# Cross attention's first loads in another order, the latent weights' split one slot later, and pair 0's mask product last

## The reference

```
xn     = layernorm(x)
scores = xn @ ctx^T / sqrt(512)         # 64 x 256 per batch
scores = where(mask, scores, -1e30)
x1     = x + softmax(scores) @ ctx      # 0 where a batch has no valid row
z      = layernorm(x1) @ [wq_a; wkv_a]^T    # latent projection, 512 -> 576
z      = z + bias, then rmsnorm and rope of its parts
```

## Time and profile before

| what | value |
|---|---|
| median of 3 runs | 1119.59 us (1118.59 to 1121.09) |
| profiled execution, first to last instruction | 1117.5 us |
| TensorE busy | 1087.1 us, 97% of the span |
| VectorE, ScalarE, GpSimd busy | 532.0, 348.9, 324.1 us |
| cross attention | about the first 130 us, slots of 8.12 us from slot 5 on |

### The profile page before, as it was taken

How to read it: one execution, slowest core, us unless ns; L and a number is a source line. 1 busy time by engine, 2 the same in 40 slices (tenths; PEclk the granted TensorE clock), 3 DMA queues, 4 the chain that set the end, 5 groups by cost and what they waited for, 6 DMA issues and landing times.

```text
span 1117.5 us, 20885 instructions
## 1 busy us (share of the span) xinstructions
PE 1087.1 (97%) x8097; PEld 948.6 (85%) x8097; DVE 532.0 (48%) x998; ACT 348.9 (31%) x698; POOL 324.1 (29%) x371
## 2 busy tenths in 40 slices
PE   5999999999999999999999999999999999999996
PEld 3677787888988898888988888889999998989895
DVE  3666556544454444434443456745344443525242
ACT  3555554322222222232222225513122222313130
POOL 2334470121212121121212122525243332415151
PEclk9999999999999999999999999999999999999998
DMA  9999942002011111102111117401010010101000
GB/s 355 414 418 381 407 184 70 22 18 75 20 42 47 42 56 41 48 19 69 30 33 56 39 52 232 170 1 39 1 39 22 17 38 0 38 0 39 1 19 19
DMA packets 41071, 100.96 MB, mean 90 GB/s; under 512 B 7289, under 2 KB 11412, under 8 KB 36532
## 3 DMA queue, kind: packets, MB, share of 16 engines
q1 hardware_dynamic: 39284, 96.62, 24.4%
q10 hardware_dynamic: 1728, 3.54, 0.8%
HBM read 74.45 MB, written 17.30 MB: 82 GB/s over the span
## 4 chain that ended last, share of the span: by engine, by line
PE 90%; DVE 3%; issue 2%; POOL 2%; DMA 1%; ACT 1%; SPq 0%; DVEq 0%; POOLq 0%; ACTq 0%
PE b_z L44 6%; PE b_z L45 6%; PE b_z L46 6%; PE b_score L44 5%; PE b_prob L46 5%; PE b_prob L44 5%; PE b_score L46 5%; PE b_score L45 5%; PE b_prob L45 5%; PE b_z L1101 3%; PE b_read L44 3%; PE b_free L44 3%; PE b_read L46 2%; PE b_read L45 2%; PE b_free L46 2%; PE b_free L45 2%
## 5 line engine op out<-in xcount | busy, mean ns | idle before, releaser
L817 POOL TENSOR_TENSOR m_e<-m_e,m_rs 128x512 f32<-128x512 f32 x32 | 34.6, 1083 | 357.8 <-DVE m_rs L972 357.8
L1447 POOL TENSOR_TENSOR f_hT_lo<-f_h,f_hT_hi 128x512 fp32r<-128x512 f32 x64 | 89.4, 1397 | 93.3 <-ACT f_hT_hi L1490 88.5
L46 PE MATMUL b_z<-m_zT_hi,m_wq_hi 128*128 128x256 f32 x384 | 108.7, 283 | 0.0
L44 PE MATMUL b_z<-m_zT_lo,m_wq_hi 128*128 128x256 f32 x384 | 108.7, 283 | 0.0
L45 PE MATMUL b_z<-m_zT_hi,m_wq_lo 128*128 128x256 f32 x384 | 108.7, 283 | 0.0
L1546 DVE TENSOR_TENSOR f_h<-f_h 128x512 f32<-128x512 f32 x64 | 72.7, 1136 | 61.4 <-ACT f_h L1485 61.4
L913 DVE TENSOR_TENSOR m_pT_lo<-b_turn,m_pT_hi 128x512 fp32r<-128x512 f32 x32 | 22.1, 692 | 160.3 <-ACT m_pT_hi L864 160.3
L858 ACT ACTIVATE m_qT<-b_z,m_q_bias 128x256 f32<-128x256 f32 x128 | 53.7, 471 | 79.0 <-PE b_z L46 75.3
L44 PEld LDWEIGHTS b_z<-m_zT_lo,m_wq_hi 128*128 128x128 f32 x384 | 73.7, 192 | 0.0
L45 PEld LDWEIGHTS b_z<-m_zT_hi,m_wq_lo 128*128 128x128 f32 x384 | 73.7, 192 | 0.0
L46 PEld LDWEIGHTS b_z<-m_zT_hi,m_wq_hi 128*128 128x128 f32 x384 | 73.7, 192 | 0.0
(11 more groups left out here) (234 smaller groups left out, 3176.9 us busy)
## 6 DMA issues: line engine op xcount, KB each, us to landing
x_ctx_in<-ctx_rows_dram SPq DMA_DIRECT2D x16, 1024.0 KB, 15.3
x_ctxT<-ctx_turned_dram SPq DMA_DIRECT2D x15, 1024.0 KB, 14.9
m_swapped<-m_by_sin SPq DMA_DIRECT2D x128, 64.0 KB, 2.0
m_raw<-attn_raw_dram SPq DMA_DIRECT2D x6, 768.0 KB, 11.0
m_z_in<-z_scratch SPq DMA_DIRECT2D x8, 576.0 KB, 3.8
x_x_all<-x_dram SPq DMA_DIRECT2D x16, 256.0 KB, 15.5
m_x<-x_scratch SPq DMA_DIRECT2D x8, 512.0 KB, 3.6
x_scratch<-m_x SPq DMA_DIRECT2D x8, 512.0 KB, 2.8
```

The source lines that it names most:

```text
L44: nc.tensor.matmul(out, lh, rl, start=first, stop=False)
L46: return nc.tensor.matmul(out, lh, rh, start=False, stop=last)
L817: q.tensor_tensor(e[:], e[:], rs[:].unsqueeze(2).broadcast_to([P, HB, SEQ]), ALU.mult).then_inc(s["normed"], 1)
L1447: g.tensor_tensor(hT_lo[:, 2 * n:2 * n + 2].rearrange("p m n -> p (m n)"), h[:, n % 2], hT_hi[:, 2 * n:2 * n + 2].bitcast(F32).rearrange(" ...
```

## The change

Three edits. SyncE issues its first loads in another order: both halves of pair 0's turned context ahead of x tile 1, x tiles 3, 4 and 5 further ahead, and the latent weights behind the turned context of pair 3. VectorE's split of the latent weights moves from the end of its slot 2 into slot 3, between latent_kv (nothing yet in slot 3) and bias(0). For pair 0 alone the mask product comes behind the 16 score products, and closes the sum in place of opening it; the wait for masks_built moves with it.

```diff
         load_x(0)
         first_ctxT(0)
+        first_ctxT(1)
         load_x(1)
-        first_ctxT(1)
         sp.dma_start(mask_u8[:], A["mask_BxS2_bk0"]).then_inc(s["masks_loaded"], 16)
         sp.wait_ge(s["pool_setup"], 2)
         sp.dma_start(picks[0:BATCH, 0:PAIRS].rearrange("p a n -> p (a n)"), A["picks"]).then_inc(s["masks_loaded"], 16)
         load_x(2)
+        load_x(3)
         load_ctxT(1)
         load_ctx(0)
-        load_x(3)
+        load_x(4)
         load_ctxT(2)
         load_ctx(1)
-        load_x(4)
+        load_x(5)
+        load_ctxT(3)
         sp.dma_start(w_raw[:], A["w_latent"].rearrange("(k p) n -> p k n", p=P)).then_inc(s["w_loaded"], 16)
-        load_ctxT(3)
         load_ctx(2)
-        load_x(5)
         sp.dma_start(small[:], A["small"]).then_inc(s["small_loaded"], 16)
...
             validate(p)
             if has(p - 4):
                 latent_kv(p - 4, par)
+            if p == 3:
+                dve.wait_ge(s["w_hi"], 1)
+                split(w_lo[:].rearrange(flat), w_raw[:].rearrange(flat), w_hi[:].rearrange(flat), s["w_lo"])
             if has(p - 3):
                 bias(p - 3, 1 - par)
             if p == PAIRS - 3:
                 w.columns(dve)
-            if p == 2:
-                dve.wait_ge(s["w_hi"], 1)
-                split(w_lo[:].rearrange(flat), w_raw[:].rearrange(flat), w_hi[:].rearrange(flat), s["w_lo"])
...
-            if p == 0:
-                pe.wait_ge(s["masks_built"], 1)
-            t.matmul(b_score[:, 0:CTX], picks[:, p].bitcast(BF16), mask_rows, start=True, stop=False)
+            if p:
+                t.matmul(b_score[:, 0:CTX], picks[:, p].bitcast(BF16), mask_rows, start=True, stop=False)
             for k in range(KH):
                 if p == 0 and k % 2 == 0:
                     pe.wait_ge(s[f"ctxT_first{k // 2}"], 16)
                 for b in range(2):
                     rows = slice(SEQ * b, SEQ * b + SEQ)
                     mm = t.matmul(b_score[rows, 0:CTX], xnT0[:, k, rows], ctxT[:, p % RING, k, CTX * b:CTX * b + CTX],
-                                  start=False, stop=k == KH - 1)
+                                  start=p == 0 and k == 0, stop=p != 0 and k == KH - 1)
+            if p == 0:
+                pe.wait_ge(s["masks_built"], 1)
+                mm = t.matmul(b_score[:, 0:CTX], picks[:, p].bitcast(BF16), mask_rows, start=False, stop=True)
             mm.then_inc(s["scored"], 1)
```

## The result

The changed kernel takes 1125.85 us (median of 6 runs, 1124.77 to 1128.98), the kernel before 1120.05 (6 runs, 1118.59 to 1121.09) beside it: a ratio of 1.0053, with an interval of 1.0042 to 1.0064. It is slower by 5.8 us, where +2.9 was forecast; the forecast range ended at 1124.8.

A forecast was written before the change was run, and what follows sets the result against it. TensorE was taken to bound the kernel, losing time only in cross attention's first four slots. Project(0) 3.6 us later, less 0.7 given back, made +2.9 on 1119.59: 1122.5 us, range 1119.8 to 1124.8.

The forecast's parts named there:

- The start: Pair 0 of cross attention: with the mask product last, score products begin near 8.6 us, a gain of about 1.8 us.
- The loads: Slots 1 and 2: context rows 2 land at 30.55, so read(2) starts at 30.6, only 0.4 us sooner.
- The split: Slot 3: w_lo waits behind residual(2), project(0) starts 3.6 us later; slot 4 gives back 0.7, so +2.9 us.
- The clock: TensorE's 4.6 us gap before project(0): a fall to half clock possible, but only when the gap is nearly over; 1.7 us.
- the likeliest case: Slot 3's lateness alone, with no price for the clock: +2.9 us, 1122.5 us, chance 0.45.
- the rival: The same lateness, and TensorE's clock falls to 1.2 GHz in the gap: +4.6, 1124.2 us, chance 0.20.
- the loads are no gate: Context rows 2 do not hold read(2), the start's whole gain reaches project(0): +1.5, 1121.1 us, chance 0.17.
- the delay is taken up: A TensorE wait at the end of cross attention hangs on the weight loads: 1119.6 us, chance 0.08.
- VectorE's relief pays: VectorE in slot 3 has w_lo ready before 35.2 us: -1.7, 1117.9 us, chance 0.10.

The follow-up runs named there:

- the late filler: 13 transposes of the identity ahead of project(15); in the changed kernel, together with 30 transposes ahead of the wait for w_lo: 1122.21 us, ratio 1.0015.
- the last version: Changed kernel with the split in slot 3 between first_var(5) and residual(2), plus 13 transposes ahead of project(15): 1118.09 us, ratio 0.9981 to the kernel before.

## Why the prediction was wrong

**The start: right.** Score products at 8.53 (8.6 forecast), turn0(1) at 12.47 (12.8), read(1) 2.0 us sooner (1.8).

**The loads: right.** Context rows 2 at 30.7 (30.55) took the gain of the start, read(2) at 30.77 (30.6); the weights at 27.9 (28.0). That they were the gate is shown by moving them: read(2) then starts at 29.02.

**The split: right, to a few hundredths.** w_lo from 35.58 (35.5), TensorE idle for 4.5 us (4.6), project(0) at 38.23 (38.2), 0.68 us given back in slot 4: +2.96 for a forecast of +2.9. The kernel with context rows 2 first and the gap filled has this lateness without the clock: project(0) at 36.27 is 1.68 late against the earlier trace rows and 1.0 after slot 4's return, and it is 1.8 us over before (1.1 to 3.1 by its interval).

**The clock: here it failed.** The step as the prediction put it: "a fall is possible, but it would come when the gap is nearly over", with a chance of 0.20, and a price of 1.7 us from a stretch of 3.5 us. It rested on one case, the end of the kernel, where the clock had held through 4.5 us of idling, and took that as typical. The runs showed a fall 2.4 us into the gap, a half clock of 6.8 us, of which 4.7 lay on real work, and a price of 2.1 us in the trace. In the times filling the gap was worth 2.3 us by the medians with context rows 2 first, 1.3 with the late filler beside it, and 0.8 alone. And it was no matter of chance: the mean granted clock of all 12 timed runs of the changed kernel was 0.990 to 0.993, and each of the four profiles with this gap unfilled (the changed kernel twice, the split alone, context rows 2 first) has the fall in it. A gap of 2 us is another matter: ahead of read(2) it brought a fall in the profile of the split back in slot 2, and none in the two of the changed kernel (idle for 2.3 and 2.5 us) nor in that of the last version (2.2); ahead of project(15) it did in six profiles of eleven. For 4.5 us the likeliest case and the rival should have been one. Lateness and clock together, 2.9 and 2.1, are 5.0; measured were 5.8 (interval 4.7 to 7.2) and 5.0 when the changed kernel was run again.

The Trainium skill says more than I took from it: TensorE: Matmul & The Clock Gate, section "HAM oscillation — how this bites in real kernels", warns that waits of 3 to 5 us between stretches of products lose the clock over and over. The traces here agree, for 4.5 us in each of four.

**The profiled execution as a base.** The prediction carried a sum from one execution over to a median. That holds for lateness, which every run has. It fails for anything that the profiled run had by luck: its clock of 0.996 against a mean of 0.9936 is an estimated one or two stretches of 3.4 us at half clock fewer than the mean, and nothing in one trace can tell that. Here the sum was added to a median (1119.59, against 1120.05 of the six runs), so this error stayed small.

**Rivals.** That the loads are no gate, that the delay is taken up, and that VectorE's relief pays are all refuted by the traces. VectorE's relief was real (the maximum of pair 3 at 28.53 in place of 34.40) and worth nothing, since its next use stood behind project(0).

## What to carry to other kernels

When an operation is moved down an engine's list, write down what the operations ahead of it wait for: the split went behind residual(2), and by that behind a product, behind a load, and then in front of 24 products that needed it. Here the place ahead of the engine's next wait cost nothing, and the one behind it cost the whole wait. Price a long idle gap of TensorE twice, once for itself and once for the products behind it at half clock (in all four profiles at 4.5 us here, at times at 2 us). Where a gap can't be closed, useless transposes in it can keep the clock: here they ended before w_lo was there and delayed nothing. And take more than one profile before a single one becomes the base of a sum.

## What was not expected of the hardware

While VectorE made w_lo, a GpSimd operation on one element per partition (line 350) took 2.57 us, against 0.27 in the other slots; it ended as the split did. The same row is there with the split alone moved. Where the split stands ahead of residual(2), it is the GpSimd operation before it that runs beside the split and is drawn out, from 0.55 to 2.70 us, while line 350 takes 0.27:

```profile
30.15 2.70 POOL L346 TENSOR_TENSOR x_rstd<-x_var_eps,m_neg_half 128x1 f32<-128x1 f32 x1 [0.36 <-DVE x_var_eps L473]
33.02 0.27 POOL L350 TENSOR_SCALAR x_shift<-x_mean_var,x_rstd 128x1 f32<-128x1 f32 x1 [0.17 <-POOL x_rstd L346]
```

It was hidden here: slot 4 of the changed kernel still takes 8.12 us. The Trainium skill has it (SBUF — State Buffer, section "SBUF: two separate sides": VectorE with two SBUF inputs and a GpSimd operation that reads SBUF exclude each other for the whole instruction), and the trace agrees: 35.58 plus 2.55 and 35.70 plus 2.57 end within 0.14 us of each other.

Open is why the transposes gave less alone (1125.06), and with the late filler, than with context rows 2 first: that falls ahead of read(2) took the rest back is argued from one profile of another kernel, and its own profile shows none.
